# Three stage borders of a four-block kernel, reordered by token tiles on one Trainium2 core

## The chip, the cores and the metric

The kernel runs on one core of a Trainium2 chip. Its time is device microseconds of one execution, from the first instruction to the last, and a kernel stands by the median of its runs. A core has five engines that each execute their own instructions in order: TensorE (PE: products and transposes; PEld is its weight load), VectorE (DVE), ScalarE (ACT), GpSimd (POOL) and SyncE (SP, which here only issues DMA transfers). They wait for each other by semaphores alone.

## The reference

Four blocks in a row on 1024 tokens (2 sequences of 512) of width 512, all float32:

```python
x = x + layernorm(L0_attn(layernorm(x)))   # Mamba2-like: in_proj, conv of 4 + silu, selective scan, out_proj
x = x + layernorm(L0_ffn(layernorm(x)))    # hidden = silu(x @ gate.T) * (x @ up.T); out = hidden @ down.T
x = x + layernorm(L1_attn(layernorm(x)))   # 32 heads of 16, causal softmax
x = x + layernorm(L1_ffn(layernorm(x)))    # mixture of 8 experts, the best 2 for each token

# L0_attn, 64 heads of 64 in G = 8 groups, state of 128
gate, hbc, dt = split(x @ in_proj.T)                      # 4096, 6144, 64 columns
xs, B, C = split(silu(conv_bias + sum_k pad(hbc)[k] * conv_w[k]))
dt = softplus(dt + dt_bias);  dA = exp(-dt * exp(A_log))
state = state * dA + (dt * xs) B;   y = state C + D * xs  # step by step over the tokens
y = rms_norm_in_groups_of_512(y) * norm_weight * silu(gate);   out = y @ out_proj.T

# L0_ffn: weights are -1, 0 or 1 (1792 x 512 gate and up, 512 x 1792 down), each row with its own scale
```

## The kernel before

*Tiling.* Tokens lie in NT = 8 tiles of P = 128, CH = 4 to a sequence (NB = 2 sequences, L = 512 tokens each). The residual stream is x (8 tiles of 128 x 512), the running output of a block acc. The normed stream, transposed, is xT, 512 rows of width in KT = 4 pieces of 128.

*Products.* Each float32 factor is split in a high part (a cast, mostly on ScalarE: names with h) and a low part (what the cast left out, made by `low`, L360: names with l). `products` (L355) makes three matmuls for each piece: high x high, high x low, low x high. The ternary feed-forward weights are exact and need two matmuls.

*Stages.* (1) Opening: norm of x, its transposes, dt, the convolutions of group 0. (2) Eight groups of the scan in a loop, `group_steps`: steps s = 0 to 7 of every group, the last group has steps 8 and 9 as well. Step s of `step(g, s, first, last)` transposes and enters token tile s, works the state and the scan of tile i = s - 1, and makes the output product of tile i - 1 (in group order: output tile s - 2), which VectorE adds to acc (L1353). In between stand the convolutions and gates of the next group, where there is one. (3) The norm of the output, residual, and the norm of that sum. (4) Feed-forward, FP = 7 pairs of 256 hidden columns: four halves for each pair (two token halves by two pieces, 16 products of 512 columns each, L1728), then down products (L1738), the sums on VectorE (`add_down`). (5) The same double norm, with the value projections of the attention behind each tile. (6) Attention and experts, which the change leaves as they are.

*Order.* Nothing is planned at run time: each engine's program is written out by hand, and the order of its lines is the order of the work. A wait at the head of an engine's queue holds all that stands behind it.

*Opening.* SP loads x, the dt weights and small parameters, then group 0's convolution weights, gate weights (when the convolution's low halves are made) and output weights. `norm_vector(0)` on VectorE and `norm_pool` on GpSimd norm a tile per round, `norm_turn` (L677) transposes it, `norm_scalar` (L687) copies the high half, `norm_low` (L641) makes the low half. ScalarE first waits for the convolution weights and copies them (L918) and the dt weights (L920), and only then copies the tiles. TensorE then does the dt products, their transposes, convolution 0, convolution 1 (`convolved`), the two cumulative sums of dt (L1697, L1700), and convolutions 2 to 5; from the fourth on a gate product (`gated`) follows each. A convolution's way out is: ScalarE's first tap (L927), three VectorE taps (L1202), ScalarE's tanh (L935), VectorE's silu (L1208). GpSimd makes the two decay tiles (`decays(0)`, L710), clears acc (L719, waiting for the last transpose) and makes the gate weights' low halves (`gate_low(0)`); ScalarE's high halves (`gate_high(0)`, L1016) come behind the tap of the third convolution. Group 0 begins with the transposes of L1606.

*End of the last group.* VectorE adds output tile i and goes straight into `norm_round(1, i)`: statistics of tile n of the output and of tile n - 2 of the residual sum, normed output n - 1 (for GpSimd to add to x), normed input n - 3 (L628) for the next stage. The transposes of these inputs (L677) stand on TensorE behind the last output product, for all eight tiles, then the first four halves. SP loads the first feed-forward weights (gur, dnr) behind the last loads of x, ScalarE casts them (L1061) after the copies of the transposed tiles, GpSimd clears acc (L792) after the last transpose, and VectorE needs that for the scales (fsc, L1362).

*End of the feed-forward stage.* The last pair is a turn of the loop like the others. `down(6, 1)` stands behind it; then come ScalarE's casts of the attention weights (L1086, L1090), GpSimd's low halves (awl), and the norm rounds from tile 0.

## Time and profile before

| | |
|---|---|
| three runs | 1735.08, 1736.45, 1738.42 us; median 1736.45 |
| profiled execution, own time | 1735.23 us |
| its span in the trace | 1733.5 us |
| busy: TensorE, VectorE, GpSimd, ScalarE | 89%, 71%, 55%, 48% |
| granted TensorE clock, mean | 0.954 |
| opening; groups; end of the last group; feed-forward; values stage; rest | 92.2; 881.8; 54.6; 159.4; 53.5; 492.0 us |

Times in the trace count from the start of its span. Busy time of TensorE is modelled from pipelined records; a granted clock of 1.00 is the upper of two levels (2.4 GHz), 0.50 the lower (1.2 GHz), and a mean between them is a mix of both. L12 is line 12 of the kernel. What stands in brackets behind an instruction is how long its engine was idle ahead of it, and what ended that.

### The profile page before, as it was taken

How to read it: one execution, taken by the hardware profiler on the slowest of the kernel's cores; microseconds unless marked ns; L12 is line 12 of the kernel's file. 1: busy time of each engine (PE TensorE's matmuls, PEld its weight loads, DVE VectorE, ACT ScalarE, POOL GpSimd, SP SyncE). 2: the span in 40 equal slices, each digit the busy share in tenths (PEclk: the TensorE clock that was granted, in tenths of full speed). 3: DMA queues.
4: the chain of work that ended last, by engine and by line, in shares of the span. 5: the costliest groups of instructions: out<-in, count | busy, mean ns of one | idle time of the engine just before them, and what ended most of it. 6: DMA issues, size and time to landing. Idle time of an engine off the chain costs nothing.

```text
span 1733.5 us, 26612 instructions
## 1 busy us (share of the span) xinstructions
PE 1551.4 (89%) x8870; PEld 1216.9 (70%) x8870; DVE 1225.2 (71%) x2024; ACT 827.2 (48%) x1639; POOL 947.4 (55%) x861
## 2 busy tenths in 40 slices
PE   3789999999999999999999869994889999987791
PEld 2567877877878778778787658883667676766681
DVE  5568878788788787877887866557467677768425
ACT  2355554554555545545545423331166667663231
POOL 3257667576676675766766851005443334427544
PEclk9899999999999999999999979997899999997796
DMA  3102111011021110120211022231000000042344
GB/s 117 37 5 87 33 49 58 17 48 64 13 86 31 48 57 16 48 67 12 89 27 48 20 80 73 73 97 36 0 14 1 14 1 2 1 171 74 122 138 165
DMA packets 49498, 92.60 MB, mean 53 GB/s; under 512 B 8017, under 2 KB 32721, under 8 KB 44177
## 3 DMA queue, kind: packets, MB, share of 16 engines
q1 hardware_dynamic: 45744, 79.58, 14.4%
q0 software_dynamic: 3680, 12.06, 2.1%
q8 instruction: 43, 0.70, 0.2%
q14 instruction: 31, 0.25, 0.0%
HBM read 81.14 MB, written 10.49 MB: 53 GB/s over the span
## 4 chain that ended last, share of the span: by engine, by line
PE 60%; DVE 15%; POOL 8%; issue 7%; ACT 5%; DMA 3%; SPq 1%; POOLq 0%; ACTq 0%; DVEq 0%
PE banks L355 29%; PE banks L1728 6%; DVE tap L1202 3%; PE banks L1854 3%; PE banks L1738 3%; PE banks L1819 2%; PE banks L1620 2%; PE banks L1652 2%; PE banks L1646 2%; DMA x<-in_w_gate 2%; PE banks L1844 2%; POOL wol L360 2%; PE banks L1661 2%; DVE acc L623 1%; DVE nmax L1440 1%
## 5 line engine op out<-in xcount | busy, mean ns | idle before, releaser
L1202 DVE SCALAR_TENSOR_TENSOR tap<-banks,parg,tap 128x511 f32<-128x511 f32 (+2 forms) x288 | 215.2, 747 | 39.0 <-ACT tap L927 31.8
L710 POOL TENSOR_TENSOR am<-ah,upto 128x1024 fp32r<-128x1024 f32 x64 | 121.9, 1905 | 187.4 <-PE banks L1620 138.2
L862 POOL TENSOR_SCALAR kz<-kst,head 128x512 fp32r<-128x512 f32 x64 | 99.1, 1567 | 159.9 <-DVE kst L1429 159.9
L355 PE MATMUL banks<-xTh,wch 128*128 128x512 f32 x384 | 162.4, 423 | 4.6 <-DVE em L1302 4.6
L935 ACT ACTIVATE th<-tap 128x512 f32<-128x512 f32 x96 | 60.7, 632 | 212.3 <-DVE tap L1202 210.2
L355 PE MATMUL banks<-xTh,wcl 128*128 128x512 f32 x384 | 150.9, 393 | 0.0
L355 PE MATMUL banks<-xTl,wch 128*128 128x512 f32 x384 | 150.0, 391 | 0.0
L1134 ACT ACTIVATE prob<-banks,nmax 128x128 f32<-128x128 f32 (+3 forms) x256 | 121.8, 530 | 54.6 <-DVE nmax L1440 54.4
L1440 DVE TENSOR_REDUCE nmax<-banks 128x2 f32<-128x256 f32 (+3 forms) x128 | 104.8, 819 | 40.3 <-PE banks L1845 40.2
L710 POOL TENSOR_TENSOR am<-al,upto 128x1024 fp32r<-128x1024 f32 x64 | 122.3, 1911 | 0.0
L1302 DVE TENSOR_TENSOR em<-banks,gmask 128x1024 f32<-128x1024 f32 x64 | 78.2, 1222 | 50.7 <-ACT banks L970 49.8
L355 PE MATMUL banks<-xTh,wgh 128*128 128x512 f32 x256 | 108.4, 424 | 5.2 <-POOL wgl L360 4.7
L1854 PE MATMUL banks<-ident,prob 128*128 128x128 f32 x640 | 95.6, 276 | 10.7 <-DVE pB L1450 7.2
L355 PE MATMUL banks<-woh,ynTh 128*128 128x512 f32 x256 | 102.7, 401 | 1.1 <-DVE acc L1353 1.1
L355 PE MATMUL banks<-xTh,wgl 128*128 128x512 f32 x256 | 101.7, 397 | 0.0
L355 PE MATMUL banks<-woh,ynTl 128*128 128x512 f32 x256 | 101.1, 395 | 0.0
L355 PE MATMUL banks<-xTl,wgh 128*128 128x512 f32 x256 | 100.9, 394 | 0.0
L355 PE MATMUL banks<-wol,ynTh 128*128 128x512 f32 x256 | 100.6, 393 | 0.0
L927 ACT ACTIVATE tap<-banks,parg 128x512 f32<-128x512 f32 x96 | 74.2, 773 | 50.9 <-PE banks L355 50.0
L355 PEld LDWEIGHTS banks<-xTh,wch 128*128 128x128 f32 x384 | 72.4, 189 | 32.9 <-DVE em L1302 10.8
L1728 PE MATMUL banks<-xTh,gu 128*128 128x512 f32 x224 | 90.0, 402 | 2.9 <-ACT gu L1061 2.8
L360 POOL TENSOR_TENSOR awl<-prob,awh 128x512 fp32r<-128x512 f32 x8 | 10.1, 1297 | 145.2 <-ACT awh L1090 132.9
(289 smaller groups left out, 4476.8 us busy)
## 6 DMA issues: line engine op xcount, KB each, us to landing
x<-grownT SPq DMA_DIRECT2D x96, 128.0 KB, 4.7
x<-in_w_conv SPq DMA_DIRECT2D x7, 1536.0 KB, 6.6
x<-in_w_gate SPq DMA_DIRECT2D x8, 1024.0 KB, 4.9
x<-in_w_out SPq DMA_DIRECT2D x8, 1024.0 KB, 4.7
eraw<-in_expert_w SPq DMA_DIRECT2D x8, 1024.0 KB, 6.9
gur<-in_ff_gu SPq DMA_DIRECT2D x7, 1024.0 KB, 4.8
x<-in_hidden SPq DMA_DIRECT2D x16, 256.0 KB, 3.9
mates<-yd SPq DMA_DIRECT2D x8, 512.0 KB, 4.5
```

Source lines behind the costliest of these rows:

```text
L355: m = nc.tensor.matmul(o, a, b, start=first and n == 0, stop=last and n == len(terms) - 1)
L710: m = pool.tensor_tensor(am[:, part, :, :], a[:, i, :].bitcast(F32).unsqueeze(2).to_broadcast([P, HG, P]), upto[:, :].unsqueeze(1).to_broa ...
L862: m = pool.tensor_scalar(kz[:, quad % 2, p2, j, :], kst[:, p2, :].bitcast(F32), head[:, j:j + 1], None, ALU.mult)
L927: nc.scalar.activation(tap[:, q % 2, :], bk(CONV_BANKS[q % 2]), ACT.Identity, bias=parg[:, CT * KC + q:CT * KC + q + 1], scale=parg[:, KC ...
L935: nc.scalar.activation(th[:, :], tap[:, q % 2, :], ACT.Tanh).then_inc(tanh_ready, 1)
L1134: e = nc.scalar.activation(prob[:, n % 2, j, 0:kw], bk(2 * (n % 2) + j)[:, 0:kw], ACT.Exp, bias=nmax[:, n % 2, j:j + 1])
L1202: nc.vector.scalar_tensor_tensor(tap[:, q % 2, sh:L], bk(CONV_BANKS[q % 2])[:, 0:L - sh], parg[:, KC * q + k:KC * q + k + 1], tap[:, q % 2 ...
L1302: nc.vector.tensor_tensor(em[:, s % 2, :, :], decayed, gmask[:, :].unsqueeze(1).to_broadcast([P, HG, P]), ALU.mult).then_inc(m_ready, 1)
L1440: nc.vector.tensor_reduce(nmax[:, n % 2, :], banks[:, 2 * (n % 2):2 * (n % 2) + 2, 0:kw], AX, ALU.max, negate=True).then_inc(max_ready, 1)
L1728: m = mat(bk(2 * w + ft), gu[:, k, ft, w, :], part[:, k, tok], start=(k == 0 and part is xTh), stop=(k == KT - 1 and part is xTl))
L1738: m = mat(bk(4 + i % 4), part[:, k, i * P:(i + 1) * P], dn[:, k, :], start=(k == 0 and part is hidh), stop=(k == 1 and part is hidl))
L1854: m = pe.transpose(bk(4 + j)[:, c * P:(c + 1) * P], prob[:, w % 2, j, c * P:(c + 1) * P], ident[:, :])
```

## The change

It edits three borders between stages; the arithmetic stays.

*Opening.* ScalarE copies token tiles 0 to 3 first, then the dt weights, then one convolution weight behind each of tiles 3 to 6. The dt weights have a semaphore of their own (`wdt_in`). VectorE's `low_dt` moves from behind the norm to ahead of the last tile. `gate_high(0)` and `gate_low(0)` come first of the group-0 work on their engines, the first gate product stands behind convolution 1, the others behind convolutions 4 and 5. GpSimd clears acc behind `decays(0)`. The copies of the skip weights move from the head of VectorE's parameter work to behind the first silu and the first gate.

*End of the last group.* TensorE has the transposes of tiles 0 to 2 at the head of step 8, tile 3 at the head of step 9, half (0, 0) behind that step's sum of squares and ahead of the state and output products, tiles 4 and 5, half (0, 1), tiles 6 and 7, halves 2 and 3. The copies and low halves follow on ScalarE (`norm_high`) and VectorE (`norm_low`); each tile has its own bank (`turned`). The weights' loads and their casts come earlier, the scale loads no longer wait for the last tile, fsc is made ahead of the norm's last rounds.

*End of the feed-forward stage.* The last pair is unrolled: down(f, 0) comes ahead of halves 2 and 3; VectorE does norm rounds 0 to 2 of the next norm within it; ScalarE casts the down weights and the attention weights in its middle.

Waits on `abo_in` and `r_in`, and on `table_ready`, are merged into `wide_in` and `list_ready`.

The diff, cut to its core:

```diff
+        def turned(q, i):
+            return bk((5, 2, 3, 0, 4, 5, 4, 5)[i] if q == 1 else i % 2)
...
# SP
-            sp.dma_start(wdt[:, :, :], w_dt).then_inc(small_in, 16)
+            sp.dma_start(wdt[:, :, :], w_dt).then_inc(wdt_in, 16)
...
-            for i in (3, 5, 6, 7):
+            for i in (3, 5):
+                grown_load(G - 1, i)
+            if STAGES >= 2:
+                sp.wait_ge(h_ready, NB * CT * G)
+                sp.dma_start(gur[:, :, :, :, :], ff_gu[0]).then_inc(gu_in, 16)
+                sp.dma_start(dnr[:, :, :], ff_dn[0]).then_inc(dn_in, 16)
+            for i in (6, 7):
                 grown_load(G - 1, i)
...
-                sp.wait_ge(h_ready, NB * CT * G)
-                sp.dma_start(gur[:, :, :, :, :], ff_gu[0]).then_inc(gu_in, 16)
-                sp.dma_start(dnr[:, :, :], ff_dn[0]).then_inc(dn_in, 16)
-                tile_done(sp, 1, NT - 1)
                 sp.dma_start(gus[:, 0, :], gate_s).then_inc(small_in, 16)
...
# VectorE, the norm
-            lag, made = 4 if q else 2, 0
+            lag, made = 4 if q else 2, CH if q == 1 else 0
+            if q == 1:
+                norm_low(q, CH)
+                made += 1
...
# TensorE, one transposed tile
-            if i >= 2:
-                norm_wait(nc.tensor, q, "lo", i - 1)
+            freed = (0, 0, 0, 0, 0, 1, 5, 6)[i] if q == 1 else i - 1
+            if freed > 0:
+                norm_wait(nc.tensor, q, "lo", freed)
...
# GpSimd
-            norm_wait(pool, 0, "tr", NT)
-            pool.memset(acc[:, :, :], 0.0).then_inc(consts, 1)
...
+            gate_low(0)
             pool.wait_ge(ah_ready, 1)
             decays(0)
-            gate_low(0)
+            norm_wait(pool, 0, "tr", NT)
+            pool.memset(acc[:, :, :], 0.0).then_inc(consts, 1)
...
# ScalarE
-            act.wait_ge(wc_in, 16)
-            for k in range(KT):
-                nc.scalar.copy(wch[:, k, :], conv_stage(0)[:, k, :]).then_inc(wc_hi, 1)
-            act.wait_ge(small_in, 16 * 7)
-            nc.scalar.copy(wdth, wdt).then_inc(wdt_hi, 1)
-            norm_scalar(0)
+            for i in range(NT):
+                norm_high(0, i)
+                if i == KT - 1:
+                    act.wait_ge(wdt_in, 16)
+                    nc.scalar.copy(wdth, wdt).then_inc(wdt_hi, 1)
+                    act.wait_ge(wc_in, 16)
+                if i >= KT - 1 and i < 2 * KT - 1:
+                    k = i - KT + 1
+                    nc.scalar.copy(wch[:, k, :], conv_stage(0)[:, k, :]).then_inc(wc_hi, 1)
...
+                if last and s == NT:
+                    for j in range(CH - 1):
+                        norm_high(1, j)
+                if last and s == NT + 1:
+                    norm_high(1, CH - 1)
...
+                if s == NT - 1 and last and STAGES >= 2:
+                    weights_high(0)
...
+            gate_high(0)
             act.wait_ge(par_ready, 1)
             first_tap(0, 0)
...
             tanh(0, 0)
+            gate_tanh(1, 1)
...
-                if q == 1:
-                    gate_high(0)
-                if q >= 3:
+                if q >= 4:
                     gate_tanh(q - 2, (1, 7)[(q - 3) % 2])
...
+                        if q == 1 and last:
+                            act.wait_ge(down_ps, NT * f)
+                            down_high(f)
+                            act.wait_ge(awr_in, 16)
+                            for k in range(KT):
+                                nc.scalar.copy(awh[:, k, :], awr[:, k, :]).then_inc(aw_hi, 1)
+                            weights(0)
...
# VectorE
+            norm_vector(0, 0, lambda n: low_dt() if n == NT - 1 else None)
...
             silu(0, 0, 0)
+            gate_made(1, 1, 0, 0)
+            for u in range(2):
+                rows = slice(HP * u, HP * u + HP)
+                nc.vector.tensor_copy(skip[rows, :, :], ...)
             dve.wait_ge(dt_act, 5)
...
+                if last and s == NT + 1:
+                    norm_low(1, CH - 1)
...
                     if last and i >= 0:
                         norm_round(1, i)
+                if last and s == NT:
+                    for j in range(CH - 1):
+                        norm_low(1, j)
             group_steps(dve, step)
+            if STAGES >= 2:
+                dve.wait_ge(small_in, 16 * 10)
+                chain(nc.vector.tensor_scalar(fsc[:, 0, :], gus[:, 0, :], 0.5, None, ALU.mult))
+                nc.vector.tensor_tensor(fsc[:, 1, :], fsc[:, 0, :], gus[:, 1, :], ALU.mult).then_inc(f_part, 1)
             norm_vector(1, NT)
...
+                def last_pair(f):
+                    dve.wait_ge(hid_ready, 4 * f)
+                    nc.vector.tensor_copy(fscg[:, :, :], fsc[:, :, 2 * f:2 * f + 2]).then_inc(fsc_ready, 1)
+                    for q in range(2):
+                        hidden(f, q, False)
+                    add_down(f - 1, 1)
+                    add_down(f, 0)
+                    norm_round(2, 0)
+                    for q in range(2, 4):
+                        hidden(f, q, False)
+                    norm_round(2, 1)
+                    norm_round(2, 2)
+                    add_down(f, 1)
...
# TensorE
+                if last and s == NT:
+                    pe.wait_ge(m_ready, NT * G)
+                    for i in range(CH - 1):
+                        norm_turn(1, i)
+                if last and s == NT + 1:
+                    norm_turn(1, CH - 1)
...
+                if last and s == NT + 1 and STAGES >= 2:
+                    norm_wait(pe, 1, "lo", CH)
+                    pe.wait_ge(gu_cast, KT)
+                    half(0, 0, True)
                 i, c = s - 1, (s - 1) % CH
...
             convolved(1, 1, 0)
+            pe.wait_ge(wg_lo, KT)
+            gated(0, 0, 1)
             pe.wait_ge(dve_step, 9)
...
+                pe.wait_ge(ssv_ready, NT * G)
+                for i in range(CH, CH + 2):
+                    norm_turn(1, i)
+                tile_done(pe, 1, NT - 1)
+                half(0, 1, True)
+                for i in range(CH + 2, NT):
+                    norm_turn(1, i)
+                norm_wait(pe, 1, "lo", NT)
+                half(0, 2, True)
+                half(0, 3, True)
+                pe.wait_ge(dn_cast, 2)
+                down(0, 0)
+                with pe.Fori(1, FP - 1) as f:
+                    hidden_pair(f)
+                f = FP - 1
+                pe.wait_ge(gu_cast, KT * f + KT)
+                half(f, 0, False)
+                half(f, 1, False)
+                down(f - 1, 1)
+                pe.wait_ge(dn_cast, 2 * f + 2)
+                down(f, 0)
+                half(f, 2, False)
+                half(f, 3, False)
+                down(f, 1)
```

## Rows read from the trace of the kernel before

**Rows 1.** The page, part 4: the chain that ended last, by engine.

```profile
PE 60%; DVE 15%; POOL 8%; issue 7%; ACT 5%; DMA 3%; SPq 1%; POOLq 0%; ACTq 0%; DVEq 0%
```

**Rows 2.** Table of stages: stretch, us; PE, PEld, DVE, ACT, POOL busy; clock; DMA; GB/s.

```profile
0.00:92.20 92.20, 50.84 (x192) 35.49 (x193) 50.58 (x83) 28.12 (x44) 25.84 (x29) 0.93 0.24 73
...
974.00:1028.60 54.60, 34.40 (x177) 26.00 (x176) 43.26 (x88) 17.59 (x39) 34.82 (x41) 0.77 0.17 54
1028.60:1188.00 159.40, 159.31 (x672) 127.53 (x672) 93.06 (x149) 57.93 (x100) 22.51 (x57) 0.98 0.21 73
1188.00:1241.50 53.50, 30.60 (x129) 23.97 (x130) 35.62 (x80) 4.70 (x8) 31.33 (x36) 0.74 0.08 30
```

**Rows 3.** Timeline, the opening's norm: start us, us, engine, line, operation [idle before].

```profile
17.68 3.03 ACT L918 CAST wch<-xbc 128x768 fp32r<-128x768 f32 x4 [15.58 <-DMA xbc<-in_w_conv]
21.53 0.69 DVE L360 TENSOR_TENSOR xTl<-banks,xTh 128x512 fp32r<-128x512 f32 x1 [7.65 <-ACT xTh L687]
36.36 1.28 DVE L360 TENSOR_TENSOR wol<-xdec,woh 128x256 fp32r<-128x256 f32 x1
37.56 5.44 DVE L1226 COPY skip<-y 64x32 f32<-64x32 f32 x2
37.78 0.66 PE L355 MATMUL banks<-xTh,woh 128*64 128x512 f32 x1 [2.69 <-DVE wol L360]
```

**Rows 4.** Timeline, the opening's products on TensorE, GpSimd's gate weights, group 0's first transposes.

```profile
56.40 1.22 PE L1697 MATMUL banks<-per,after 128*128 128x512 f32 x1 [5.13 <-DVE per L1244]
67.56 5.50 POOL L360 TENSOR_TENSOR wgl<-x,wgh 128x512 fp32r<-128x512 f32 x4 [6.89 <-ACT wgh L1016]
73.11 0.79 PE L355 MATMUL banks<-xTh,wgh 128*128 128x512 f32 x1 [4.73 <-POOL wgl L360]
92.20 1.09 PE L1606 MATMUL banks<-ident,xbc 128*128 128x128 f32 x4 [2.61 <-DVE xbc L1208]
```

**Rows 5.** Timeline, VectorE in the opening's convolutions.

```profile
58.98 2.24 DVE L1208 SCALAR_TENSOR_TENSOR xbc<-th,tap 128x512 f32<-128x512 f32 x1
68.80 0.68 DVE L1208 SCALAR_TENSOR_TENSOR xbc<-th,tap 128x512 f32<-128x512 f32 x1
70.39 2.31 DVE L1202 SCALAR_TENSOR_TENSOR tap<-banks,parg,tap 128x511 f32<-128x511 f32 x3 [0.91 <-ACT tap L927]
```

**Rows 6.** Timeline, VectorE at the end of the last group: normed inputs and output tiles.

```profile
999.52 0.54 DVE L628 TENSOR_SCALAR acc<-x,mv,rs 128x512 f32<-128x512 f32 x1
1005.29 0.74 DVE L1353 SCALAR_TENSOR_TENSOR acc<-banks,rg,acc 128x512 f32<-128x512 f32 x1
1010.75 0.75 DVE L1353 SCALAR_TENSOR_TENSOR acc<-banks,rg,acc 128x512 f32<-128x512 f32 x1 [2.08 <-PE banks L355]
1017.08 0.54 DVE L628 TENSOR_SCALAR acc<-x,mv,rs 128x512 f32<-128x512 f32 x1
```

**Rows 7.** Timeline, GpSimd: the accumulator's memset behind the last transpose.

```profile
1025.80 3.51 POOL L792 MEMSET acc<- 128x4096 f32 x1 [4.76 <-PE banks L677]
```

**Rows 8.** Stretches within the last group's step 6, same columns as rows 2.

```profile
977.00:981.00 4.00, 3.89 (x24) 3.66 (x26) 3.97 (x10) 0.26 (x1) 4.00 (x3) 0.50 0.00 0
```

**Rows 9.** Chain of waits in order of time: start us, us, what.

```profile
977.70 1.92 PE banks L1646 x8
979.61 1.91 PE banks L1652 x16
...
1026.26 2.18 ACT gu L1061 x4
...
1028.58 17.51 PE banks L1728 x64
```

**Rows 10.** Timeline, GpSimd and VectorE where the norm behind the feed-forward begins.

```profile
1182.64 5.08 POOL L360 TENSOR_TENSOR awl<-prob,awh 128x512 fp32r<-128x512 f32 x4 [132.91 <-ACT awh L1090]
...
1191.49 0.69 DVE L612 BATCH_NORM_STATS2 stats<-acc 128x6 f32<-128x512 f32 x1 [2.84 <-POOL acc L847]
...
1202.53 0.53 DVE L628 TENSOR_SCALAR acc<-x,mv,rs 128x512 f32<-128x512 f32 x1
```

More of the change, by code:

```diff
@@ L653, in norm_vector @@
                     after(n)
-                while q < STAGES and made <= n - lag and made < (NT if n == NT + lag - 1 else 2 * (n - start) + 2):
+                while q < STAGES and made <= n - lag:
                     norm_low(q, made)
@@ L1086, in weights, with down_high, hidden_pair @@
                         nc.scalar.copy(aqh[:, w, :, :], aqr[:, w, :, :]).then_inc(aq_hi, 1)
-                act.wait_ge(awr_in, 16)
-                for k in range(KT):
-                    nc.scalar.copy(awh[:, k, :], awr[:, k, :]).then_inc(aw_hi, 1)
-                weights(0)
+                def down_high(f):
+                    act.wait_ge(dn_in, 16 * f + 16)
+                    for k in range(2):
+                        nc.scalar.copy(dn[:, k, :], dnr[:, k, :]).then_inc(dn_cast, 1)
+                def hidden_pair(f, first, last=False):
+                    if not first:
+                        act.wait_ge(up_ps, 4 * f)
+                        weights_high(f)
+                    act.wait_ge(fsc_ready, f + 1)
+                    for q in range(4):
+                        act.wait_ge(gate_ps, 4 * f + q + 1)
+                        nc.scalar.activation(fth[:, q % 2, :], bk(q % 2), ACT.Tanh,
+                                             scale=fscg[:, 0, q % 2:q % 2 + 1]).then_inc(f_tanh, 1)
+                        if q == 2 and not last:
+                            down_high(f)
+                        if q % 2:
+                            for r in (q - 1, q):
+                                act.wait_ge(hid_f, 4 * f + r + 1)
+                                nc.scalar.copy(hid_part(hidh, r), hidf[:, r % 2, :]).then_inc(hid_hi, 1)
+                        if q == 1 and last:
+                            act.wait_ge(down_ps, NT * f)
+                            down_high(f)
+                            act.wait_ge(awr_in, 16)
+                            for k in range(KT):
+                                nc.scalar.copy(awh[:, k, :], awr[:, k, :]).then_inc(aw_hi, 1)
+                            weights(0)
+                hidden_pair(0, True)
+                with act.Fori(1, FP - 1) as f:
+                    hidden_pair(f, False)
+                hidden_pair(FP - 1, False, True)
+            if STAGES >= 3:
                 norm_scalar(2)
@@ L1221, in chain @@
                 dve.wait_ge(dve_step, d.n)
-            for u in range(2):
-                rows = slice(HP * u, HP * u + HP)
-                nc.vector.tensor_copy(skip[rows, :, :], skip_in[rows, :].rearrange("p (g k u) -> p g k u", k=KT, u=2)[:, :, :, u])
             chain(nc.vector.tensor_scalar(par[:, :, :], par[:, :, :], 0.5, None, ALU.mult))
@@ L1411, in values @@
                                             abv[:, :].rearrange("p (h d) -> p h d", h=AH), ALU.add).then_inc(v_f, 1)
[L1413 removed]
+                norm_vector(2, 3, lambda n: values(n - 6) if n >= 6 else None)
                 for i in range(NT - 2, NT):
@@ L1592, in gated, with half @@
                                     for k in range(KT)]).then_inc(gate_ready, 1)
+            def half(f, q, first):
+                b, ft = q // 2, q % 2
+                tok = slice(b * L, (b + 1) * L)
+                if not (first and q < 2):
+                    pe.wait_ge(hid_f, 4 * f + q - 1)
+                for w, done in ((0, gate_ps), (1, up_ps)):
+                    for k in range(KT):
+                        for part in (xTh, xTl):
+                            m = mat(bk(2 * w + ft), gu[:, k, ft, w, :], part[:, k, tok],
+                                    start=(k == 0 and part is xTh), stop=(k == KT - 1 and part is xTl))
+                    m.then_inc(done, 1)
             def step(g, s, first, last):
@@ L1713, in _ @@
             if STAGES >= 2:
-                tile_done(pe, 1, NT - 1)
-                norm_tensor(1)
-                norm_wait(pe, 1, "lo", NT)
-                def gate_up(f, b, first):
-                    tok = slice(b * L, (b + 1) * L)
-                    for ft in range(2):
-                        q = 2 * b + ft
-                        if not (first and q < 2):
-                            pe.wait_ge(hid_f, 4 * f + q - 1)
-                        for w, done in ((0, gate_ps), (1, up_ps)):
-                            for k in range(KT):
-                                for part in (xTh, xTl):
-                                    m = mat(bk(2 * w + ft), gu[:, k, ft, w, :], part[:, k, tok],
-                                            start=(k == 0 and part is xTh), stop=(k == KT - 1 and part is xTl))
-                            m.then_inc(done, 1)
                 def down(f, b):
```

147 lines of the change are left out of this document (63 added, 84 removed).

## The prediction

> **What bounds the kernel now.** I read the chain that ended last first: TensorE holds most of it [rows 1]. Then the table of stages [rows 2], whose second column is TensorE's busy time. The feed-forward products leave TensorE nothing (159.3 of 159.4 us), so an edit there can only shift them. The three stages that the change edits are the loose ones: the opening has TensorE busy 50.8 of 92.2 us, the end of the last group with the norm behind it 34.4 of 54.6, the norm and values stage behind the feed-forward 30.6 of 53.5, the last two at a granted clock near three quarters. What the change can win lies in those holes. All sums below stand against the profiled execution: span 1733.5 us, its own time 1735.2, the median of the three runs 1736.45. I work out a difference and take it from the median.
>
> **Opening, the norm.** ScalarE waits for the group-0 weights until 17.68, copies them for 3 us, and only then copies transposed tiles; VectorE, which wants tile 0's copy, stands idle 7.65 us [rows 3]. The change copies tiles 0 to 3 first and threads each weight copy (3.03/4 = 0.76 us) between later tiles. VectorE then runs on from 13.9 with its own pace of 1.9 us a tile, into which 0.6 + 0.76 us of ScalarE fits: 7.5 us gone. The low half of the dt weights, which VectorE made last (1.28 us), moves ahead of the last tile and out of the way: 1.0. The first product starts at 37.8 - 8.5 = 29.3. That its weights wait on a counter of their own costs nothing: they are issued before the big load.
>
> **Opening, the products.** TensorE stands idle 5.13 us before the cumulative products and 4.73 us before the first gate product, which waits for GpSimd's low halves of the gate weights [rows 4]. After such a hole its clock is at 1.2 GHz (0.50 in the rows of step 6 [rows 8]), so the 12 products behind it, 512 columns each, cost 12 × 512 / 1.2 GHz = 5.1 us and not 2.85 (0.237 us each in the feed-forward stage [rows 2]). The change makes the gate weights before everything else (ScalarE's copies at about 37, GpSimd's 5.5 us at 37.5 to 43), puts the first gate product into the 5.13 us hole, and so removes the 4.73 us wait and most of 5.1 us from TensorE's queue. What is late next is VectorE. It is free for the third convolution only after: decays' input at 56.4 - 8.5 + 0.5 = 48.4 (half a microsecond for one VectorE operation of that chain held by GpSimd's low halves), GpSimd's two decay operations, the accumulator's memset now behind them, 3.5 us [rows 7], and the skip copies, which were held 5.44 us by just such neighbours and now stand on VectorE's path: 48.4 + 3.8 + 3.5 + two copies, one multiply = 57.2. From there each tile takes ScalarE's tap 0.91 (with its wait), three VectorE operations 2.31 and the silu 0.68 [rows 5], 3.9 us: third convolution 57.2, fourth 61.1, fifth 65.0, sixth 69.3 (TensorE is 0.4 late for it), then 2.3 + 0.7 + 1.5 to the last silu: 73.5. Group 0 starts at 73.7, not at 92.2: **18.5 us**. If TensorE's clock falls in the 2 us gap before the fifth convolution, 2.4 us for each refill of two or so: 15; if VectorE slips ahead of the memset, 21. Queues passed: SP issues the same loads in the same order, w_out[0] no later than its turn at 73 before; ScalarE's gate copies lie before the first tap, which waits for TensorE until 39 anyway.
> The Trainium skill (SBUF — State Buffer, section "SBUF: two separate sides") says that VectorE and GpSimd share a port pair as an exclusive lock, and that a VectorE operation with two SBUF inputs is held only by a GpSimd operation that reads SBUF. This trace agrees for the decays: a silu took 2.24 us beside one. By that rule the first silu slips ahead of the memset and only the skip copies wait; were it held too, the sum would be 0.7 us smaller.
>
> **End of the last group.** This part loses. TensorE executes in order, and the change puts transposes of tiles 0 to 2 at the head of step 8 and tile 3 at the head of step 9. Tile 2's input leaves VectorE at 1000.1 [rows 6], in the round that ends step 7; TensorE is through with step 7 at about 995.8. So TensorE stops 3.6 us there, and queued behind are the sum of squares, the state products and the products of tile 7, on which VectorE, ScalarE and output tile 6 wait. The hole drops the clock: at 1.2 GHz the products in question took 1.92 + 1.91 us [rows 9]. Output tile 6 is added at 1005.3 before; after: 1000.1 + 1.1 transposes + 0.4 + 3.8 + VectorE and ScalarE's chain of 4.3 = 1009.8, 4.5 later. The same again in step 9: tile 3's input comes with that round, 2.6 us later, then its copy, the low halves of tiles 0 to 3 on VectorE until 1015.9, the first feed-forward half (16 products: 3.8 us at full clock, 6.0 behind a hole, most of them at 1.2 GHz), and only then output tile 7 (2.8): added at 1021 to 1025, not 1010.75, **10.3 to 14.3 later**.
> From that point the old kernel needed 1046.1 - 1011.5 = 34.6 us to the end of the first four halves [rows 6, 9]. The new: tile 5's input 5.6 to 6.1 us later [rows 6], the second half 3.8 to 6.0, transposes of tiles 6 and 7 1.1 to 1.9 (tile 7's input is there by then): last transpose at 10.5 to 14. Now a chain that was covered is open: the third half waits for the first hidden tile, that for the scales on VectorE behind the memset of the accumulator (3.51 us on GpSimd, which starts only after the last transpose), then tanh, two VectorE operations. Before, the memset ran beside the first half. 3.5 + 0.2 + 0.7 + 0.7 + 0.75 and hand-overs = 6.2 us, in which TensorE stands, so the two halves behind cost 6.0 + 3.8: in all 26.5 to 30. Against 34.6 that is 4.6 to 8.1 us back. Sum of this part: **2 to 10 us lost, 7 taken** (both stops at the lower clock, the first half short of it in part).
> Covered edits: the feed-forward weights' loads now stand on SP ahead of the last two decay loads, but are issued near 962, when the queue has nothing else, and land 5 us later; ScalarE's four casts of them (2.18 us [rows 9]) move into step 7, where it waits for VectorE; without that cover they would delay step 8's copies, which wait longer for tile 2. The small scale loads leave the wait for the last tile: nothing waited for them.
>
> **End of the feed-forward stage.** The last pair does the first token half's down products before the last two halves, so norm tiles 0 to 2 start early; ScalarE casts the next stage's weights in the middle, GpSimd's low halves (5.08 + 2.5 us) end near 1182.5 instead of 1190.2, and the first norm statistics come at 1183.8 instead of 1191.49 [rows 10]. But VectorE does them ahead of hidden tiles 2 and 3: these wait to 1184.9, the last down products start at 1189.5 instead of 1184, and VectorE adds their results before round 3. Round by round: round 1 at 1189.4, round 2 to 1195.0 (GpSimd's chain of rstd, residual, scale), adds to 1197.5, input of transpose 0 at 1199.9 instead of 1203.06. After that the pace of 4.7 us a round is unchanged. **3.1 us won**; 2 if the last down products run at the low clock and the adds wait for them, 4.5 if the rounds close up.
>
> **Sum.** -18.5 + 7 - 3.1 = -14.6. 1736.45 - 14.6 = 1721.9 (the profiled execution: 1720.6).
>
> **The rivals.** *The entry is hidden*: VectorE's rounds, not TensorE, set the end of the group, so the stops cost nothing beyond the 3 us: -18.5 + 0 - 3.1 (entry taken as even), and 1715; for it, GpSimd is busy 34.8 of 54.6 us there; against it, every wait I listed sits on the in-order queue. *The opening gives less*: the shared port or the clock holds the new order, 12 to 14 us; with the entry at 9 the sum is 13 - 9 + 3 = 7: 1729. For it, the 5.44 us copy; against it, the gate wait goes in any case. *The clock does not come back* (slower): the change cuts TensorE's work at the entry into pieces with stops between, and the stage stays at 1.2 GHz until the first pair is through. Then the four halves cost 27.3 instead of 17.5, output tiles 5 us more, and the opening's last four blocks 9 more: the entry loses 19, the opening gives 11, the values stage, eight tiles of 6.2 us of TensorE instead of a 4.7 us round, loses another 12 less the 3: +17, 1753; it turns slower once the low clock costs 14.6 us in all. For it, the granted clock of 0.77 and 0.74 in the two stages; against it, the low stretches in the trace end soon after dense products resume, as behind 1028.58, where 64 products took 17.5 us and not 27.3 [rows 9].
> The Trainium skill (TensorE: Matmul & The Clock Gate, "HAM oscillation — how this bites in real kernels") says that stops between bursts of products send the clock back to half each time; that is this rival at its full length, and the trace agrees for single stops.
>
> **Chances.** Forecast 62%, entry hidden 13%, opening less 15%, clock stays low 5%, else 5%. The range takes in the two middle rivals and the bounds of the three terms (best 21 + 4.5 - 2 = 23.5, worst 15 + 2 - 10 = 7): 1712 to 1731. About 0.2% (3.5 us) is what a measurement of this kernel tells from no change. Faster by more 89%, within it 5%, slower 6%.
>
> **What the changed profile would show.** Right: VectorE's first idle of 7.65 us gone, group 0's first transposes near 74, no gate wait; two TensorE stops of 3 to 4 us at the heads of steps 8 and 9, a memset on the chain that ended last ahead of the third half, and the first four halves ending about 10 us earlier, not 18, by the clock of the span. Wrong: no stop in step 8; the memset off the chain; group 0 starting after 78; statistics of the norm behind the feed-forward not before the last down products.

## The result

The changed kernel took 1723.61 us, the median of four runs (1719.94 to 1724.12), against 1737.12 us for the kernel before beside it (1735.08 to 1738.42). The ratio is 0.9917, 95% interval 0.9904 to 0.9930: 14.4 us less (12.2 to 16.7). The forecast was 14.6 less, in a range of 5 to 24. The profiled execution of the changed kernel is its fastest (own time 1719.94, span 1718.2); the three others took 3 to 4 us more.

The stages of the changed kernel, to be read beside rows 2: the opening to the start of group 0, the groups, the end of the last group, the halves behind it, the rest of the feed-forward, the norm and values, the rest. Columns are the stretch, its length, busy time of TensorE, of its weight loads, of VectorE, ScalarE and GpSimd, the granted clock, DMA share and GB/s.

```profile
0.00:73.97 73.97, 48.20 (x193) 33.62 (x193) 49.57 (x83) 28.24 (x44) 25.89 (x29) 0.97 0.29 90
73.97:955.90 881.93, 868.00 (x4773) 696.10 (x4773) 700.28 (x1045) 465.75 (x906) 614.36 (x522) 1.00 0.15 46
955.90:1015.00 59.10, 39.75 (x188) 31.19 (x189) 38.99 (x86) 15.40 (x35) 30.77 (x39) 0.77 0.14 41
1015.00:1034.50 19.50, 13.35 (x54) 10.71 (x53) 8.61 (x14) 6.49 (x11) 13.54 (x33) 0.81 0.08 28
1034.50:1176.50 142.00, 138.42 (x593) 110.37 (x591) 83.80 (x135) 52.40 (x91) 18.28 (x31) 1.00 0.24 82
1176.50:1230.00 53.50, 37.15 (x160) 28.73 (x161) 36.78 (x84) 7.89 (x14) 29.71 (x34) 0.87 0.00 0
1230.00:1718.20 488.20, 405.86 (x2915) 306.32 (x2914) 301.36 (x582) 250.93 (x540) 214.10 (x177) 0.91 0.18 62
```

The opening is 92.20 - 73.97 = 18.2 us shorter, with almost the same busy time of TensorE (48.2 against 50.8 [rows 2]): what went were holes, and products at the lower clock. The groups are as long as before: VectorE adds the last group's output tile 5 904.3 us behind group 0's start, 904.9 before (such a length differs by up to 5 us between the traces below). The fourth half ended at 1046.09 before [rows 9] and ends at 1034.53 now, 11.6 us earlier: of the 18.2 us, 6.7 are gone by there. TensorE's idle times on this stretch, from its timeline, are new ones. In brackets stands the idle time ahead of the instruction and what ended it; L687 are the transposes of normed tiles, L1667 the halves.

```profile
981.31 1.12 PE L687 MATMUL banks<-ident,acc 128*128 128x128 f32 x4 [3.47 <-DVE acc L634]
...
992.99 1.11 PE L687 MATMUL banks<-ident,acc 128*128 128x128 f32 x4 [4.34 <-DVE acc L634]
...
1008.41 0.90 PE L687 MATMUL banks<-ident,acc 128*128 128x128 f32 x4 [3.16 <-DVE acc L634]
1012.22 1.11 PE L687 MATMUL banks<-ident,acc 128*128 128x128 f32 x4 [2.90 <-DVE acc L634]
...
1025.07 0.76 PE L1667 MATMUL banks<-xTh,gu 128*128 128x512 f32 x1 [6.15 <-DVE hidf L1433]
```

The first two are the stops at the heads of steps 8 and 9 (tiles 2 and 3, forecast 3.6 and the same again), the next two the waits for tiles 4 and 5, the last is the one ahead of the third half (forecast 6.2). The chain that ended last, in order of time (start, us, what), runs from the last transposes through the memset to the third half (pieces of under 0.1 us are left out):

```profile
1013.34 4.71 PE banks L1667 x16
1018.05 0.89 PE banks L687 x8
1018.99 3.52 POOL acc L804
1022.53 0.18 DVE fscg L1443
1022.74 0.70 ACT fth L1108
1023.46 0.70 DVE fh L1429
1024.18 0.76 DVE hidf L1433
1024.94 0.14 issue
1025.07 9.46 PE banks L1667 x32
```

At the other end, the first product of the attention's query and key projections starts at 1224.42 and not at 1241.38. From the fourth half's end that is 189.9 us and 195.3 before: the last border gives 5.4 us. The remaining 1.7 us to the difference of the spans (15.3) are lost behind it, 1.5 of them in the output projection of the attention, whose granted clock was 0.92 in the profile of after and 1.00 in that of before. The change edits nothing there. The whole stretch from that product to the end took 491.4 to 494.2 us in the thirteen traces of this document, and 491.4 to 491.8 in three variants that contain the change's opening and end, so the 1.7 are not a price of those; why the clock was lower was not looked into.

### The profile page after: what moved, and what is told of

Read it like the earlier page. It is cut to its first block, busy times and chain, and to the rows that moved or that the text cites. A ratio compares the mean times of both kernels' runs of the same rounds, so it can differ in the third digit from the quotient of the medians.

```text
span 1718.2 us, 26565 instructions
## 1 busy us (share of the span) xinstructions
PE 1550.7 (90%) x8870; PEld 1217.0 (71%) x8870; DVE 1219.4 (71%) x2024; ACT 827.1 (48%) x1639; POOL 946.7 (55%) x861
## 3 DMA queue, kind: packets, MB, share of 16 engines
q1 hardware_dynamic: 45744, 79.58, 14.4%
## 4 chain that ended last, share of the span: by engine, by line
PE 61%; DVE 16%; POOL 8%; issue 7%; ACT 5%; DMA 3%; SPq 0%; POOLq 0%; DVEq 0%; ACTq 0%
PE banks L360 29%; PE banks L1667 6%; DVE tap L1239 3%; PE banks L1944 3%; PE banks L1807 3%; PE banks L1909 2%; PE banks L1739 2%; PE banks L1733 2%; PE banks L1703 2%; DMA x<-in_w_gate 2%; PE banks L1934 2%; POOL wol L365 2%; PE banks L1748 2%; DVE acc L629 1%; DVE nmax L1505 1%
## 5 line engine op out<-in xcount | busy, mean ns | idle before, releaser
L1944 PE MATMUL banks<-ident,prob 128*128 128x128 f32 x640 | 95.8, 276 | 10.6 <-DVE pB L1515 7.2
L1667 PE MATMUL banks<-xTh,gu 128*128 128x512 f32 x224 | 92.4, 413 | 7.6 <-DVE hidf L1433 6.1
L1667 PE MATMUL banks<-xTl,gu 128*128 128x512 f32 x224 | 91.0, 406 | 0.0
```

Of the source, the lines that this page charges most:

```text
L1667: m = mat(bk(2 * w + ft), gu[:, k, ft, w, :], part[:, k, tok], start=(k == 0 and part is xTh), stop=(k == KT - 1 and part is xTl))
L1944: m = pe.transpose(bk(4 + j)[:, c * P:(c + 1) * P], prob[:, w % 2, j, c * P:(c + 1) * P], ident[:, :])
```

## The experiments

All eleven were timed in five rounds beside the kernel before. A gain below is what the ratio lacks to 1, times 1737. Two lengths are read from the trace of each and are steadier than its time, since the length of the groups, with the same instructions, varies by up to 5 us between the traces (903.8 to 908.9 from group 0's start to output tile 5): *entry*, from the addition of output tile 5 to the end of the fourth half, and *end*, from there to the first query and key product. In the five traces that leave the entry as it was, its length is 48.6 to 49.3. *Group 0* is the time of its first transposes.

| kernel | median us | ratio (95%) | group 0 | entry | end |
|---|---|---|---|---|---|
| before | 1737 | 1 | 92.2 | 49.0 | 195.3 |
| changed | 1723.6 | 0.9917 (0.9904 to 0.9930) | 74.0 | 56.3 | 189.9 |
| opening alone | 1718.6 | 0.9895 (0.9879 to 0.9912) | 74.4 | 49.3 | 195.3 |
| entry alone | 1747.0 | 1.0058 (1.0041 to 1.0076) | 94.1 | 58.2 | 194.1 |
| end alone | 1732.1 | 0.9976 (0.9966 to 0.9986) | 94.6 | 48.7 | 190.0 |
| changed without entry | 1713.4 | 0.9869 (0.9852 to 0.9886) | 74.1 | 49.1 | 189.9 |
| norm of the opening alone | 1726.5 | 0.9952 (0.9939 to 0.9966) | 83.0 | 49.0 | 195.3 |
| changed, scales early | 1722.5 | 0.9915 (0.9897 to 0.9933) | 74.0 | 56.2 | 190.0 |
| changed, half behind | 1717.2 | 0.9889 (0.9872 to 0.9907) | 74.8 | 49.0 | 189.8 |
| changed, calm order (last group ordered by when tiles come) | 1711.1 | 0.9846 (0.9826 to 0.9866) | 74.1 | 45.7 | 190.0 |
| changed, memset early in the opening | 1722.6 | 0.9923 (0.9904 to 0.9941) | 74.0 | 56.0 | 189.8 |
| changed, scales' copy early | 1717.8 | 0.9891 (0.9875 to 0.9907) | 73.4 | 52.3 | 190.1 |
| calm order, scales' copy early, three moves more | 1700.4 | 0.9798 (0.9782 to 0.9814) | 74.0 | 38.7 | 189.4 |

**The three parts, each alone, and the change without its second part.** The edit is the diff shown above, cut at the three borders.

> The kernel before with the change's opening alone. By my sum, and by the trace of the changed kernel (group 0 starts at 73.97 and not at 92.20), 18.2 us faster: 1737 becomes 1719, group 0 starts near 74 and everything behind it is shifted whole. Rival: the gain is given back in the groups (loads or the in-order queues that the new phase collides with), then 10 to 14 us.

> The kernel before with the reordered end of the last group alone. By my sum 7 us slower (1744): two stops of TensorE of 3 to 4.5 us at the heads of steps 8 and 9, a third of 5 to 6 us ahead of the third half with the memset on it. Rival: VectorE's rounds set the end of the group in any order and the part is even or faster (1737 or less).

> The kernel before with the unrolled last pair alone. By my sum 3 us faster (1734); by the trace of the changed kernel, where the value stage ends 5.2 us earlier than the two other parts explain, up to 5 us (1732). Rival: it only works with the other parts' phases, then no change.

> The changed kernel with the end of the last group put back: opening and last pair only. If the three parts add up, 7 us faster than the changed kernel: 1737 - 18 - 4 = 1714 to 1716. If the entry is even, the same as the changed kernel (1723).

The opening gives 18.2 us (15.3 to 21.0) and the end 4.2 (2.4 to 5.9); the entry costs 10.1 (7.1 to 13.2) alone, and its entry length is 9.2 us longer than before. Without it the changed kernel is faster: 0.9869, whose interval does not meet that of the changed kernel. In entry length the part costs 56.3 - 49.1 = 7.2 us. The rivals of these runs (the gain given back in the groups, the entry even, the end worth nothing without the other parts) fall. The sum of the three taken alone is 12.3 us less, beside 14.4 less measured together: they add up within their intervals.

**Half of the opening.** The order of copies, with the low half of the dt weights ahead of the last tile, is kept; everything about the gate weights, the memset and the skip copies is put back.

```diff
-            gate_high(0)
             act.wait_ge(par_ready, 1)
...
-            pe.wait_ge(wg_lo, KT)
-            gated(0, 0, 1)
             pe.wait_ge(dve_step, 9)
```

> The kernel before with the norm's part of the opening alone (token tiles copied first, weight copies between them, dt weights' low half ahead of the last tile). By my sum 8.5 us faster (1728.5), the first product starts at 29.3 and not at 37.8; the gate weights' part then is worth the other 9.5 to 10. Rival: what follows waits for the convolution weights' low halves on GpSimd, which come no earlier, then less than 5.

8.3 us (5.9 to 10.6), where 8.5 was forecast. TensorE's idle times in the opening, from its timeline:

```profile
28.74 0.69 PE L360 MATMUL banks<-xTh,woh 128*64 128x512 f32 x1 [1.40 <-DVE xTl L365]
...
64.41 0.79 PE L360 MATMUL banks<-xTh,wgh 128*128 128x512 f32 x1 [4.74 <-POOL wgl L365]
...
83.02 1.09 PE L1668 MATMUL banks<-ident,xbc 128*128 128x128 f32 x4 [2.61 <-DVE xbc L1237]
```

The first product is 9.0 us earlier than before (37.78 [rows 3]), the gate product still has its wait of 4.7 us (4.73 [rows 4]), and group 0 starts 9.2 us earlier. The other half of the part, with that wait gone, is 83.0 - 74.0 = 9.0.

**Is the memset of the accumulator on the chain ahead of the third half?**

```diff
                 dve.sem_inc(down_added, 4)
-                dve.wait_ge(consts, 8)
...
+                    if first:
+                        dve.wait_ge(consts, 8)
                     add_down(f, 0)
```

> The changed kernel, with VectorE's wait for the accumulator's memset moved from ahead of the scales to ahead of the first sum that needs it. My theory has the memset (3.51 us) on the chain ahead of the third half: its hole of 6.15 us shrinks to about 2 and the two halves behind run nearer the upper clock: 4 to 6 us faster than the changed kernel (1717 to 1719). Rival: the hole is the wait for the low halves of tiles 6 and 7 and for the tanh chain, the memset is beside it: no change (1723).

Nothing changed: the entry length is 56.2, the hole 5.97 us. By the expectation's own terms the rival had won; the rows say otherwise. VectorE and GpSimd at that place, from the timelines of this run:

```profile
1021.12 1.29 DVE L365 TENSOR_TENSOR xTl<-banks,xTh 128x512 fp32r<-128x512 f32 x2 [4.04 <-ACT xTh L696]
1022.33 2.17 DVE L1442 COPY fscg<-fsc 128x4 f32<-128x4 f32 x1
```

```profile
1020.97 3.51 POOL L804 MEMSET acc<- 128x4096 f32 x1 [4.47 <-PE banks L687]
```

A copy of 128 x 4 elements lasted 2.17 us and ended at 1024.50, with the memset (1024.48), though it no longer waited for it. The calm order below has the same 2.17 us beside its memset. The two subtractions beside the same memset took 1.29 us together, as in the changed kernel. So the memset kept its place on the chain without a semaphore: what was said at the start, that the engines wait for each other by semaphores alone, does not hold for this copy. The next run puts that copy ahead of the norm's last rounds and changes nothing else against this one (the lines that go are left out here):

```diff
                 nc.vector.tensor_tensor(fsc[:, 1, :], fsc[:, 0, :], gus[:, 1, :], ALU.mult).then_inc(f_part, 1)
+                dve.wait_ge(f_part, 1)
+                nc.vector.tensor_copy(fscg[:, :, :], fsc[:, :, 0:2]).then_inc(fsc_ready, 1)
             norm_vector(1, NT)
```

> The run with early scales showed VectorE's small copy of the scales lasting 2.17 us instead of 0.16, to the end of GpSimd's memset, with no wait between them. Here the first copy stands ahead of the norm's last rounds, and the memset's wait ahead of the first sum. If the memset held VectorE's copy through something the two engines share, the hole ahead of the third half shrinks from 6.0 to about 3.5 and the four halves end 2 to 4 us earlier than in the changed kernel (1719 to 1721). Rival: the chain from the low halves of tile 7 through tanh takes the hole's length anyway, then 0 to 1 us (1722 to 1723).

The copy takes 0.17 us, and TensorE's wait ahead of the third half, from its timeline, is half of what it was:

```profile
1011.43 0.17 DVE L1409 COPY fscg<-fsc 128x4 f32<-128x4 f32 x1
```

```profile
1025.19 0.47 PE L1669 MATMUL banks<-xTh,gu 128*128 128x512 f32 x1 [3.03 <-DVE hidf L1433]
```

3.03 and not 6.15 us; the entry length falls by 4.0, the time from 0.9917 to 0.9891 of before (4.5 us; the two intervals just overlap). Against the run with early scales, which differs by this copy alone, the entry length falls by 3.9: 2.9 are the hole (5.97 to 3.03) and 0.8 the two halves behind it (9.99 to 9.16 us, granted clock 0.74 and 0.81). That the memset reached the chain through this copy is shown. Of the hole's 2.9 us, 2.0 are the time for which the copy was held (2.17 to 0.17); the rest is that tanh no longer waits for the two subtractions ahead of the copy, which no run separates. The Trainium skill (SBUF — State Buffer, section "SBUF: two separate sides") says that VectorE in a two-port mode and GpSimd take a shared port pair as an exclusive lock, for the whole instruction; both kinds of row agree, the copy that is held and the subtraction with one operand in PSUM that is not. That the engines meet at a port, and that this copy runs in such a mode, no run here shows; what the runs show is that the copy does not end before the memset does.

**Does what stands ahead of output product 7 delay the end of the group?** The first half is moved from step 9 to behind the group; no other line moves.

```diff
-                if last and s == NT + 1 and STAGES >= 2:
-                    norm_wait(pe, 1, "lo", CH)
-                    pe.wait_ge(gu_cast, KT)
-                    half(0, 0, True)
...
+                norm_wait(pe, 1, "lo", CH)
+                pe.wait_ge(gu_cast, KT)
+                half(0, 0, True)
                 pe.wait_ge(ssv_ready, NT * G)
```

> The changed kernel, with the first half moved from ahead of output product 7 to behind it. My theory: what stands ahead of output product 7 on TensorE's in-order queue delays VectorE's rounds 7 to 10: output tile 7 is added 5 to 7 us earlier and the four halves end 4 to 6 us earlier (1717 to 1719). Rival: the half has to be done anyway and fills TensorE's wait, so that the order of the two is even (1722 to 1724).

Yes: the entry length is 49.0 and not 56.3, 7.3 us, more than expected (time: 4.9; the two intervals just overlap). Output tile 7, from VectorE's timelines of the changed kernel and of this run:

```profile
1005.29 0.75 DVE L1395 SCALAR_TENSOR_TENSOR acc<-banks,rg,acc 128x512 f32<-128x512 f32 x1 [9.56 <-PE banks L360]
```

```profile
1001.99 0.75 DVE L1395 SCALAR_TENSOR_TENSOR acc<-banks,rg,acc 128x512 f32<-128x512 f32 x1 [3.44 <-PE banks L360]
```

Counted from output tile 5 of the same execution it comes at 27.0 us in the changed kernel and at 20.8 here, 6.2 earlier. (In three other variants with the changed kernel's order up to there it comes at 25.5 to 25.7, so that 4.7 to 6.2 is the fair range.) VectorE's idle time of 9.56 us, the largest of the entry, is now 3.44. Four norm rounds hang on that tile; the half's inputs are there already, and what hangs on it, the first hidden tile, is first needed by the third half.

This run keeps both stops of TensorE, from its timeline:

```profile
984.16 1.12 PE L687 MATMUL banks<-ident,acc 128*128 128x128 f32 x4 [3.47 <-DVE acc L634]
...
995.82 1.12 PE L687 MATMUL banks<-ident,acc 128*128 128x128 f32 x4 [4.34 <-DVE acc L634]
```

Its entry is as long as that of the kernel before all the same (49.0 and 49.0). So the rest of the new order gives back what its stops cost, and the loss of the changed kernel's entry is as large as what the first half costs ahead of output product 7.

**What the entry costs without stops.** The diff is cut to the banks and TensorE; ScalarE's copies and VectorE's low halves move with the transposes, and the wait for the memset is moved as in the run with early scales.

```diff
-            return bk((5, 2, 3, 0, 4, 5, 4, 5)[i] if q == 1 else i % 2)
+            return bk((5, 2, 3, 0, 4, 5, 6, 7)[i] if q == 1 else i % 2)
...
                 if last and s == NT:
                     pe.wait_ge(m_ready, NT * G)
-                    for i in range(CH - 1):
+                    for i in range(CH - 2):
                         norm_turn(1, i)
                 if last and s == NT + 1:
-                    norm_turn(1, CH - 1)
+                    norm_turn(1, CH - 2)
...
+                norm_turn(1, CH - 1)
+                norm_wait(pe, 1, "lo", CH)
+                pe.wait_ge(gu_cast, KT)
+                half(0, 0, True)
                 pe.wait_ge(ssv_ready, NT * G)
```

> The changed kernel with the end of the last group ordered by when tiles come: transposes of tiles 0 and 1 at the head of step 8, tile 2 at the head of step 9, tile 3 and the first half behind output product 7, tiles 6 and 7 in banks of their own, and the memset's wait moved as in the run with early scales. My theory (stops of TensorE at the heads of steps 8 and 9 are the loss): no stop of more than 1 us at these places, the four halves end 15 to 24 us earlier than in the changed kernel, 1700 to 1708. Rival (VectorE's and GpSimd's rounds set the end of the group): not more than the two single moves give, 1712 to 1715.

The two stops for tiles are gone, from TensorE's timeline (the transposes at the head of step 8 without a wait, the largest wait of that step, and the one of step 9, for sums that GpSimd adds, which the kernel before has too, 2.26 us there):

```profile
981.11 1.03 PE L687 MATMUL banks<-ident,acc 128*128 128x128 f32 x8
981.98 0.28 PE L1723 MATMUL banks<-ones,y 128*128 128x1 f32 x2
982.73 1.16 PE L1732 MATMUL banks<-xbc,state 128*128 128x128 f32 x8 [0.47 <-DVE ynTl L365]
...
990.48 0.38 PE L1723 MATMUL banks<-ones,y 128*128 128x1 f32 x2 [2.17 <-POOL y L738]
```

The time is 12.3 us under the changed kernel's (0.9846; 1711), between what my two accounts had (1700 to 1708, and 1712 to 1715); the entry length falls by 10.6 and not by 15 to 24. Of the 10.6, 7.3 are the half behind output product 7, which this order contains; taking the stops away, with banks of their own for tiles 6 and 7, is worth 3.3. So the theory of this run, that the stops are the loss, had the smaller item for the whole. The hole ahead of the third half was still 5.97 us, with the held copy in it, and TensorE still waited 2.91 us for tile 5, behind VectorE's rounds.

**Is the opening's memset on VectorE's path, as my sum had it?**

```diff
+            norm_wait(pool, 0, "tr", NT)
+            pool.memset(acc[:, :, :], 0.0).then_inc(consts, 1)
             gate_low(0)
             pool.wait_ge(ah_ready, 1)
             decays(0)
-            norm_wait(pool, 0, "tr", NT)
-            pool.memset(acc[:, :, :], 0.0).then_inc(consts, 1)
```

> The changed kernel with the opening's memset of the accumulator moved on GpSimd from behind the decays to ahead of the gate weights, where GpSimd waits 5.9 us. My sum of the opening had it on VectorE's path to the third convolution: then 2 to 3.5 us faster. Rival, from the changed trace (the third convolution's products end at 56.7 us, its tap starts at 56.8, the multiply of VectorE ends at 56.9): TensorE sets that time as well, and the move gives nothing (within 1 us).

No: 0.9923, and group 0 starts at 73.98 as before the move. VectorE in the changed kernel, then in this run:

```profile
53.63 2.61 DVE L1294 COPY skip<-y 64x32 f32<-64x32 f32 x2
56.25 0.69 DVE L1296 TENSOR_TENSOR per<-per 128x512 f32<-128x512 f32 x1
57.71 0.75 DVE L1239 SCALAR_TENSOR_TENSOR tap<-banks,parg,tap 128x511 f32<-128x511 f32 x1 [0.77 <-ACT tap L943]
```

```profile
53.64 0.36 DVE L1294 COPY skip<-y 64x32 f32<-64x32 f32 x2
54.01 0.69 DVE L1296 TENSOR_TENSOR per<-per 128x512 f32<-128x512 f32 x1
57.73 2.32 DVE L1239 SCALAR_TENSOR_TENSOR tap<-banks,parg,tap 128x511 f32<-128x511 f32 x3 [3.02 <-ACT tap L943]
```

The copies fall from 2.61 to 0.36 us, VectorE is through 2.24 us earlier, and waits 3.02 instead of 0.77: VectorE's tap starts at 57.7 in both. It follows ScalarE's tap (56.8 in both), and that follows the third convolution's products on TensorE, which end just ahead of it.

**All together.** The calm order with the scales' copy early, and besides, in part:

```diff
# ScalarE: the first tanh ahead of the copies of tiles 6 and 7
+                if i == CH + 1:
+                    act.wait_ge(fsc_ready, 1)
+                    act.wait_ge(gate_ps, 1)
+                    nc.scalar.activation(fth[:, 0, :], bk(0), ACT.Tanh, scale=fscg[:, 0, 0:1]).then_inc(f_tanh, 1)
...
# VectorE: the first hidden tile within the norm's last rounds
-            norm_vector(1, NT)
+            norm_vector(1, NT, lambda n: hidden(0, 0, True) if n == NT + 2 else None)
...
# VectorE, last pair
+                    hidden(f, 2, False)
                     norm_round(2, 0)
-                    for q in range(2, 4):
-                        hidden(f, q, False)
+                    hidden(f, 3, False)
```

> All that the runs so far point to: the calm order of the last group with the scales' copy early, ScalarE's first tanh and VectorE's first hidden tile ahead of tiles 6 and 7, and, in the last feed-forward pair, hidden tile 2 ahead of norm round 0. Against the calm order alone (1711), by my theory (the hole of 5.97 us ahead of the third half is the held copy and the chain behind it): 4 to 6 us from the hole and its low clock, 1 from the last pair: 1704 to 1707. Rival: the hole is refilled by the copies and low halves of tiles 6 and 7 and the clock stays low: 1709 to 1711.

1700.4 us, 0.9798 of before: 35 us less, and by the ratios 21 less than the changed kernel, more than was expected. Against the calm order the entry length falls by 7.0, the end by 0.6. What each of the three added moves gives was not run apart. The hole ahead of the third half closed to 1.56 us, and the two halves behind it took 7.6 us and not 10.1, at a granted clock of 1.00 and not 0.73.

## Why the prediction was right, and where it was not

**The opening** (forecast 18.5, measured 18.2). The first product was forecast at 29.3 and came at 28.64; group 0 at 73.7 and came at 73.97. From first product to group 0 the sum had 44.4 us and the trace 45.3: two small errors that cancel. (The sum's last step is also added up 0.3 short: 69.3 + 2.3 + 0.7 + 1.5 is 73.8 and not 73.5.) One step of it was wrong without a price: the third convolution's tap was built on VectorE (57.2, with 3.5 us of memset). It began at 56.8 on ScalarE, and TensorE's products set it: VectorE was free at 56.9, ahead of its own part at 57.7, and with the memset moved away it was free 2.24 us earlier and nothing else moved. That the forecast came near this time is luck. The rows bear out which VectorE operations the prediction took to be held: the first silu beside the decays took 2.23 us and ended at 53.1, while the memset ran from 52.5 to 56.0; the skip copies beside the memset took 2.61, and a multiply with one operand in PSUM beside the same memset 0.68.

**The entry** (forecast 7 lost, measured 7.2 in entry length inside the changed kernel, 10 alone). The two stops, their cause (tile 2 and tile 3 ahead of their rounds) and the clock behind them came as written: a stretch behind each has granted clocks of 0.61 and 0.55 in the trace of the changed kernel (ahead of the second lies a further wait of 1.46 us).

```profile
981.30:985.70 4.40, 4.39 (x31) 3.99 (x31) 1.02 (x5) 1.90 (x6) 1.25 (x3) 0.61 0.00 0
995.80:1002.50 6.70, 6.70 (x17) 5.29 (x18) 0.00 (x0) 0.00 (x0) 1.98 (x3) 0.55 0.00 0
```

Output tile 7 was forecast 10.3 to 14.3 us later. It was added at 1006.04, that is 932.07 from group 0's start, where it stood at 919.3 before [rows 4, 6]: 12.8 later. From there to the fourth half's end 28.5 us were needed, forecast 26.5 to 30, 34.6 before. The hole ahead of the third half was 6.15, forecast 6.2. Here the mechanism was half right. The memset is on the chain, but not only through VectorE's wait: with the wait taken away, the held copy keeps it there. I had weighed such holding in the opening alone. And the loss was put on the stops and on the half together. The run with the half behind keeps both stops and loses nothing against the kernel before; the half ahead of output product 7 accounts for the 7.3 us alone.

**The end** (forecast 3.1, between 2 and 4.5; measured 5.4 in the trace, 4.2 (2.4 to 5.9) in time). This term was mis-sized. Moved by the 11.6 us, the first statistics came at 1183.9 (forecast 1183.8), the last down products at 1189.2 (1189.5), the adds ended at 1196.7 (1197.5), tile 0's input at 1198.7 (1199.9): 4.3 won by there, 1.2 more than forecast. Then the step that the pace of 4.7 us a round is unchanged failed. Transposes and first value product of the changed kernel:

```profile
1187.34 1.08 PE L687 MATMUL banks<-ident,acc 128*128 128x128 f32 x4 [5.74 <-DVE acc L634]
1191.92 1.12 PE L687 MATMUL banks<-ident,acc 128*128 128x128 f32 x4 [3.50 <-DVE acc L634]
1196.60 1.12 PE L687 MATMUL banks<-ident,acc 128*128 128x128 f32 x4 [3.56 <-DVE acc L634]
1197.37 0.78 PE L360 MATMUL banks<-awh,xTh 128*128 128x512 f32 x1
```

The first value products took 4.15 us here (to 1201.52) and 5.43 before (1213.24 to 1218.67), where they pushed the fourth transpose back by 1.3 us: the rest of the excess of 2.3. That the clock came back earlier because TensorE had worked until 1181.6 is argued from the rows alone; no run separates it.

**The sum and the rivals.** Between the two profiles it is 18.2 - 6.7 + 5.4 - 1.7 = 15.2, the difference of their spans (15.3) but for rounding; the 6.7 are 7.2 of entry length less the 0.6 by which the groups were shorter, rounded. By the ratio of the times it is 14.4. That the forecast of 14.6 came out so close is in part luck: the end gave 2.3 us more than it had, and the rest of the kernel 1.7 less. *The entry is hidden* fell with the run of the entry alone; *the opening gives less* fell with the opening alone; *the clock does not come back* fell too: the granted clock of the feed-forward behind the four halves is 1.00. The time that the first rival had for an even entry, 1715, is what the changed kernel without its entry shows: 1713.

## What to carry to other kernels

What interleaving work into an in-order queue costs shows in what is queued behind it: ask of every moved instruction when its input leaves the engine that makes it, and what then comes later. A piece on which much hangs, like output tile 7 with its four rounds, goes ahead of work that only has to be done some time; here that was worth 7.3 us, and the order without the two stops 3.3 more. A wait taken away may free nothing if one engine's instruction still holds the other's: look for small VectorE copies that end exactly with a GpSimd instruction, and move the copy.

## What the runs showed of the hardware

A VectorE copy of 128 x 4 elements, 0.17 us by itself, lasted 2.17 us beside a GpSimd memset of 3.51 us, which reads nothing, and ended with it, in two kernels; two skip copies fell from 2.61 to 0.36 us when the memset was moved. Subtractions and multiplies with one operand in PSUM ran at their own 0.65 to 0.69 us beside the same memsets. With the same instructions, the addition of the seventh group's last output tile came 835.0 to 839.2 us behind group 0's start in the thirteen profiled executions, 4.2 us apart, which hides edits of one or two microseconds unless a stage is measured for itself.
